# Interleaving the steps of a fixed-point feed-forward over three rows on VectorE and ScalarE

## The reference, cut to what matters

```
def float2fix(x, mantissa_bits):
    s = jnp.float32(2.0 ** mantissa_bits)
    q = jnp.round(x * s) / s
    return x + jax.lax.stop_gradient(q - x)

def pwlin_gelu_basic(x, mantissa_bits_in, mantissa_bits_out):
    xq = float2fix(x, mantissa_bits_in)
    y = jnp.interp(xq, _PWL_X, _PWL_Y)
    y = jnp.where(xq > 4.0, xq, jnp.where(xq < -4.0, jnp.float32(0.0), y))
    return float2fix(y, mantissa_bits_out)
h = jnp.einsum('bsd,df->bsf', x, w1) + b1
h = float2fix(h, 8)
h = pwlin_gelu_basic(h, 8, 8)
h = float2fix(h, 8)
out = jnp.einsum('bsf,fd->bsd', h, w2) + b2
return float2fix(out, 8)
...
x = x + _L1_ffn_ref(_layernorm(x, axis=-1), L1_ffn_w1, L1_ffn_b1, L1_ffn_w2, L1_ffn_b2)
return x
```

## Time and profile before

| | before |
|---|---|
| median of 3 runs | 2263.24 us (2263.04 to 2269.09) |
| the profiled execution | 2266.41 us |
| its span, first to last instruction | 2264.6 us |
| mean granted TensorE clock | 0.933 |
| busy share PE / DVE / ACT / POOL | 87% / 72% / 44% / 30% |
| the block that the change touches, with the store | 2126.3 to 2264.6 us of the span |

### The profile page before, as it was taken

One profiled execution on the slowest core, in us unless ns is written; L12 is line 12 of the kernel. 1 busy time (PEld: TensorE's weight loads), 2 busy tenths in 40 slices (PEclk: granted clock), 3 DMA queues, 4 the chain that ended last, 5 costly groups with the idle time before them and its releaser, 6 DMA issues. The chain is left out here.

```text
span 2264.6 us, 44140 instructions
## 1 busy us (share of the span) xinstructions
PE 1973.3 (87%) x17797; PEld 1085.4 (48%) x17800; DVE 1633.7 (72%) x2842; ACT 994.9 (44%) x1404; POOL 679.4 (30%) x704
## 2 busy tenths in 40 slices
PE   4799999999588356899999999999999999767896
PEld 1355555555445222355555555555555555434542
DVE  4399999999654794477777777777777776446676
ACT  2399998989410321233333333333333333202332
POOL 1344454444310450023332333333333332121010
PEclk8899999999699567999999999999999999988898
DMA  4133322332120401000000000000000000110400
GB/s 141 51 91 94 94 72 70 94 95 57 29 112 31 171 0 37 21 22 21 21 21 21 21 21 22 21 21 21 22 21 22 21 2 2 48 70 0 154 0 19
DMA packets 40091, 106.16 MB, mean 47 GB/s; under 512 B 19281, under 2 KB 21585, under 8 KB 33745
## 3 DMA queue, kind: packets, MB, share of 16 engines
q1 hardware_dynamic: 39888, 103.35, 14.8%
HBM read 75.42 MB, written 1.05 MB: 34 GB/s over the span
## 5 line engine op out<-in xcount | busy, mean ns | idle before, releaser
L1352 POOL TENSOR_SCALAR a1c_p_hi<-a1c_pf 128x512 f16<-128x512 f32 x272 | 201.6, 742 | 666.0 <-ACT a1c_pf L1408 623.5
L403 POOL TENSOR_SCALAR a0c_p_hi<-a0c_r 128x1024 f16<-128x1024 f32 x128 | 154.6, 1208 | 282.4 <-DVE a0c_r L492 279.5
L1377 ACT ACTIVATE a1c_k_hi<-PS 128x512 f16<-128x512 f32 x136 | 81.2, 597 | 326.8 <-PE PS L1214 326.8
L497 DVE TENSOR_TENSOR a0c_p_lo<-a0c_r,a0c_p_hi 128x1024 f16<-128x1024 f32 x128 | 202.4, 1581 | 0.9 <-POOL a0c_p_hi L403 0.9
L1557 DVE TENSOR_TENSOR a1c_p_lo<-a1c_pf,a1c_p_hi 128x512 f16<-128x512 f32 x272 | 198.2, 730 | 6.0 <-POOL a1c_p_hi L1352 6.0
L1408 ACT ACTIVATE a1c_pf<-PS,a_maskc 128x512 f32<-128x512 f32 x256 | 175.1, 686 | 48.9 <-PE PS L1719 39.0
L1384 ACT ACTIVATE a1c_v_hi<-PS 128x512 f16<-128x512 f32 x136 | 81.6, 600 | 258.8 <-PE PS L1224 206.0
L1500 DVE CUSTOM_DVE_ANT_0 a1c_junk<-PS,a1c_maskr 128x512 bf16<-128x512 f32 x256 | 175.8, 687 | 18.4
L492 DVE TENSOR_TENSOR a0c_r<-PS,a0c_r 128x1024 f32<-128x1024 f32 x128 | 155.3, 1213 | 24.9 <-ACT a0c_r L452 24.7
L1475 DVE SCALAR_TENSOR_TENSOR a1c_k_lo<-PS,a1c_k_hi 128x512 f16<-128x512 f32 x136 | 93.8, 689 | 106.3 <-ACT a1c_k_hi L1377 106.3
L1482 DVE SCALAR_TENSOR_TENSOR a1c_v_lo<-PS,a1c_v_hi 128x512 f16<-128x512 f32 x136 | 94.0, 691 | 86.7 <-ACT a1c_v_hi L1384 85.3
(11 more groups left out here) (357 smaller groups left out, 4791.7 us busy)
## 6 DMA issues: line engine op xcount, KB each, us to landing
a_cf<-in_ctxT SPq DMA_DIRECT2D x16, 1024.0 KB, 5.2
a0c_ks<-a0c_k_hi SPq DMA_DIRECT2D x128, 128.0 KB, 2.4
a1c_cf<-in_ctx SPq DMA_DIRECT2D x16, 1024.0 KB, 4.8
a0c_ks<-a0c_k_lo SPq DMA_DIRECT2D x64, 128.0 KB, 2.4
f_w<-in_w SPq DMA_DIRECT2D x4, 1024.0 KB, 8.7
f_w<-in_w SPq DMA_DIRECT2D x1, 4096.0 KB, 19.8
s1q_w<-in_L1a_wT SPq DMA_DIRECT2D x3, 1024.0 KB, 7.6
w_gate_raw<-in_w_gate SPq DMA_DIRECT2D x1, 2816.0 KB, 9.5
```

The costliest lines, as they stand in the source:

```text
L403: nc.gpsimd.tensor_scalar(p_hi[:, u % 4, :], r[:, u % 4, :], 1.0, 0.0, ALU.mult, ALU.add)\
L497: nc.vector.tensor_tensor(p_lo[:, u % 4, :], r[:, u % 4, :], p_hi[:, u % 4, :], ALU.subtract)\
L1352: nc.gpsimd.tensor_scalar(p_hi[:, v % 4, :], pf[:, v % 2, :], 1.0, 0.0, ALU.mult, ALU.add)\
```

## The change

It rewrites the feed-forward's block:

- Slots: `u` gets four, the other four tiles three. TensorE now runs `output` four rows behind `hidden` (`LAG`), and signals `outputs` after each batch of the last row.
- VectorE's list is three parts that belong to three rows. `whole(n - 2)` is the last step of row n - 2, `segment(n)` the first four of row n, `between(n - 1)` the middle three of row n - 1.
- ScalarE's list in step n: `grid(n + 1)` (scale and bias), `ends(n)` (two GELUs and, new, a Relu that makes the excess over the table), `nearest(n - 1)` (rounding).
- GpSimd's 16 steps go away: `u` is held in units of a segment (`ONE / GRID`), so that one VectorE step (`K`, L2166) both shifts and rounds, and the GELUs take off the rounding constant by their bias. VectorE's `max` goes away (now the Relu). So a row has 8 steps on VectorE instead of 9, 5 on ScalarE instead of 4, none on GpSimd.
- VectorE treats each output batch as soon as its own matmul is done, and SyncE stores each batch on its own, 256 KB each, in the same block. The block with the one store is gone; the clearing of semaphores now comes after the store.

```
-                for f in range(FT1 + 3):
+                        if f == FT1 - 1:
+                            mm.then_inc(outputs, 1)
+                for f in range(FT1 + LAG):
                     if f < FT1:
                         hidden(f)
-                    if f >= 3:
-                        output(f - 3)
+                    if f >= LAG:
+                        output(f - LAG)
...
+                def grid(f):
+                    act.wait_ge(product, f + 1)
+                    if f >= 4:
+                        act.wait_ge(y_done, f - 3)
+                    nc.scalar.activation(u[:, f % 4, :], g.PS[:, f % 4, :], ACT.Identity, bias=b1s[:, f:f + 1],
+                                         scale=ONE / GRID).then_inc(u_done, 1)
+                def ends(f):
+                    i = f % 3
+                    act.wait_ge(k_done, f + 1)
+                    if f >= 3:
+                        act.wait_ge(y_done, f - 2)
+                    nc.scalar.activation(g0[:, i, :], k[:, i, :], ACT.Gelu, scale=0.25, bias=low[:, 0:1])\
+                        .then_inc(g0_done, 1)
+                    nc.scalar.activation(g1[:, i, :], k[:, i, :], ACT.Gelu, scale=0.25, bias=high[:, 0:1])\
+                        .then_inc(g1_done, 1)
+                    nc.scalar.activation(u[:, f % 4, :], u[:, f % 4, :], ACT.Relu, scale=GRID, bias=knee[:, 0:1])\
+                        .then_inc(hm_done, 1)
+                def nearest(f):
+                    act.wait_ge(y4_done, f + 1)
+                    nc.scalar.activation(g0[:, f % 3, :], g0[:, f % 3, :], ACT.Copy, scale=ONE, bias=ROUND)\
+                        .then_inc(yr_done, 1)
+                grid(0)
+                act.wait_ge(based, 3)
+                for n in range(FT1 + 1):
+                    if n + 1 < FT1:
+                        grid(n + 1)
+                    if n < FT1:
+                        ends(n)
+                    if n >= 1:
+                        nearest(n - 1)
...
-                for f in range(FT1):
-                    i = f % R
-                    pool.wait_ge(c_done, f + 1)
-                    nc.gpsimd.tensor_scalar(k[:, i, :], c[:, i, :], 1.0 / 64, -31.5 / 64, ALU.mult, ALU.add)\
-                        .then_inc(ka_done, 1)
...
+                def segment(f):
+                    U, C, K = u[:, f % 4, :], c[:, f % 3, :], k[:, f % 3, :]
...
+                    nc.vector.tensor_scalar(K, C, -31.5 / GRID, ROUND, ALU.add, ALU.add).then_inc(k_done, 1)
...
+                for n in range(FT1 + 2):
+                    if n >= 2:
+                        whole(n - 2)
+                    if n < FT1:
+                        segment(n)
+                    if 1 <= n <= FT1:
+                        between(n - 1)
+                dve.wait_ge(biased, 2)
                 for b in range(B):
+                    dve.wait_ge(outputs, b + 1)
...
+            @block.sync
+            def _(sp):
+                for b in range(B):
+                    sp.wait_ge(x_done, b + 1)
+                    sp.dma_start(out[b], g.x[:, b, :]).then_inc(stored, 16)
+                sp.wait_ge(stored, 16 * B)
```

More of the change, by code:

```diff
@@ L2029, in _, with fixed_point_ffn_1 @@
                             normalise((n - 6) // 2)
-def fixed_point_ffn_1(nc, g, d):
+def fixed_point_ffn_1(nc, g, d, out):
+    GRID = 64.0
+    GROUND = ROUND / GRID
     ONE = 256.0
+    LAG = 4
     with ExitStack() as ctx:
@@ L2043, in fixed_point_ffn_1 @@
         w1, w2 = m.sb("w1", [P, KT, F1]), m.sb("w2", [P, FT1, D])
-        b1, b1s, b2, b2s, quarter = m.sb("b1", [P, FT1]), m.sb("b1s", [P, FT1]), m.sb("b2", [P, D]), m.sb("b2s", [P, D]), m.sb("quarter", [P, 1])
+        b1, b1s, b2, b2s = m.sb("b1", [P, FT1]), m.sb("b1s", [P, FT1]), m.sb("b2", [P, D]), m.sb("b2s", [P, D])
+        low, high, knee = m.sb("low", [P, 1]), m.sb("high", [P, 1]), m.sb("knee", [P, 1])
         w2_in, b_in = m.sem("w2_in"), m.sem("b_in")
@@ L2053, in fixed_point_ffn_1 @@
         y = m.sb("y", [P, FT1, D])
-        R = 2
-        u, c, k, g0, g1 = (m.sb(n, [P, R, D]) for n in ("u", "c", "k", "g0", "g1"))
+        u = m.sb("u", [P, 4, D])
+        c, k, g0, g1 = (m.sb(n, [P, 3, D]) for n in ("c", "k", "g0", "g1"))
         o = m.sb("o", [P, B, D])
-        based, product, u_done, h_done, c_done, ka_done, k_done, t_done = (m.sem(n) for n in (
-            "based", "product", "u_done", "h_done", "c_done", "ka_done", "k_done", "t_done"))
+        based, biased, product, u_done, h_done, c_done, k_done, t_done = (m.sem(n) for n in (
+            "based", "biased", "product", "u_done", "h_done", "c_done", "k_done", "t_done"))
         g0_done, g1_done, rise_done, td_done, y4_done, yr_done, hm_done, y_done = (m.sem(n) for n in (
             "g0_done", "g1_done", "rise_done", "td_done", "y4_done", "yr_done", "hm_done", "y_done"))
-        outputs, o_done, or_done, x_done = m.sem("outputs"), m.sem("o_done"), m.sem("or_done"), m.sem("x_done")
+        outputs, o_done, or_done, x_done, stored = (m.sem(n) for n in ("outputs", "o_done", "or_done", "x_done", "stored"))
         with nc.Block() as block:
+            @block.sync
[4 more added lines that the diff above has]
+                sp.wait_ge(stored, 16 * B)
             @block.tensor
@@ L2090, in _ @@
             @block.scalar
             def _(act):
-                act.wait_ge(based, 3)
[L2093 to L2114, removed]
-                for f in range(FT1):
-                    first(f)
-                    ends(f)
-                    last(f)
+                act.wait_ge(biased, 1)
+                def grid(f):
[4 more added lines that the diff above has]
+                                         scale=ONE / GRID).then_inc(u_done, 1)
@@ L2120, in _ @@
             @block.gpsimd
             def _(pool):
-                nc.gpsimd.memset(quarter[:], 0.25).then_inc(based, 1)
-                for f in range(FT1):
-                    i = f % R
-                    pool.wait_ge(c_done, f + 1)
-                    nc.gpsimd.tensor_scalar(k[:, i, :], c[:, i, :], 1.0 / 64, -31.5 / 64, ALU.mult, ALU.add)\
-                        .then_inc(ka_done, 1)
+                nc.gpsimd.memset(low[:], -ROUND / 4).then_inc(based, 1)
+                nc.gpsimd.memset(high[:], 0.25 - ROUND / 4).then_inc(based, 1)
@@ L2131, in _ @@
                 dve.wait_ge(b_in, 32)
[L2132 to L2136, removed]
+                nc.vector.tensor_scalar(b1s[:], b1[:], ONE / GRID, None, ALU.mult).then_inc(biased, 1)
@@ L2143, in _ @@
-                    nc.vector.tensor_scalar(C, U, 1024.0, -1024.0, ALU.min, ALU.max).then_inc(c_done, 1)
+                    if f >= 3:
+                        dve.wait_ge(td_done, f - 2)
+                    nc.vector.tensor_scalar(C, U, 1024.0 / GRID, -1024.0 / GRID, ALU.min, ALU.max)\
+                        .then_inc(c_done, 1)
                     dve.wait_ge(c_done, f + 1)
-                    nc.vector.tensor_scalar(U, U, 1024.0, None, ALU.max).then_inc(hm_done, 1)
-                    dve.wait_ge(ka_done, f + 1)
@@ L2149, in _ @@
-                    nc.vector.tensor_scalar(K, K, ROUND, ROUND, ALU.add, ALU.subtract).then_inc(k_done, 1)
+                    if f >= 3:
+                        dve.wait_ge(g1_done, f - 2)
+                    nc.vector.tensor_scalar(K, C, -31.5 / GRID, ROUND, ALU.add, ALU.add).then_inc(k_done, 1)
                     dve.wait_ge(k_done, f + 1)
-                    nc.vector.scalar_tensor_tensor(out=C, in0=K, scalar=-64.0, in1=C, op0=ALU.mult, op1=ALU.add)\
-                        .then_inc(t_done, 1)
@@ L2154, in _, with between @@
-                    dve.wait_ge(g0_done, f + 1)
+                    nc.vector.scalar_tensor_tensor(out=C, in0=K, scalar=ROUND, in1=C, op0=ALU.subtract,
+                                                   op1=ALU.subtract).then_inc(t_done, 1)
+                def between(f):
+                    C, G0, G1 = c[:, f % 3, :], g0[:, f % 3, :], g1[:, f % 3, :]
                     dve.wait_ge(g1_done, f + 1)
@@ L2224, in program @@
             clear_semaphores(nc)
[L2225 to L2233, removed]
+        self_attention_1(nc, g, d)
+        clear_semaphores(nc)
+        fixed_point_ffn_1(nc, g, d, out)
+        clear_semaphores(nc)
 def laid_out(inputs):
```

19 lines of the change are left out of this document (8 added, 11 removed).

## The result

| | before | with the change |
|---|---|---|
| median of the runs | 2263.20 us (2263.04 to 2269.09, 4 runs) | 2243.44 us (2239.24 to 2247.14, 4 runs) |
| the profiled execution | 2266.41 us | 2244.46 us |
| its span | 2264.6 us | 2242.6 us |
| mean granted clock | 0.933 | 0.935 |

The ratio is 0.9906, interval 0.9882 to 0.9930: faster by about 21 us. The forecast of 2245.7 (ratio 0.9923) lies in the interval; but 0.9906 of the time before is 2241.9, just under the lower end, 2242.5, of the range.

The account below looks back on a forecast made before the run. The prediction took the row's cross-engine chain (7.11 us) as the bound, with TensorE's 6.87 next. Its terms, -13.4 - 2.6 - 0.85 + 0.9 - 1.6 = -17.5 us, took 2263.24 to 2245.7 us, range 2242.5 to 2251.

Parts of the forecast that it names:

- What bounds the kernel: Feed-forward loop: the chain over VectorE, GpSimd and ScalarE, 7.11 us a row, bounds it; TensorE's two groups, 6.87, come next.
- The loop, -13.4: Hidden and output matmuls: TensorE runs back to back, groups 3.433 us apart, ending at 2238.35 instead of 2251.76.
- VectorE's row: VectorE's eight steps per row plus the 0.7 us wait for ScalarE's rounding, summed to 5.47 us, under TensorE's 6.87.
- The tail: Last rows: y 15 ready at 2233.8, its output group due at 2234.9, so it holds by 1.1 us.
- rival (a): Last groups: VectorE or ScalarE 10 to 20% slower, TensorE waits; 2 to 4.5 us lost, about 2249; chance 0.09.
- Closing steps by batch, -2.6: VectorE's closing steps: the first batch's matmul is done three quarters of a group before the end, saving 2.6 us.
- The store: End of the kernel: last store of 256 KB lands in 2.7 us, between bounds 2.4 (128 KB) and 4.3 (1 MB).
- -0.85 + 0.9 - 1.6: Store: engines' meeting and clearing leave the path ahead (-0.85), return behind it (+0.9), smaller last store lands sooner (-1.6).
- the 0.4 + 0.9 reckoned: Behind the store's landing: 0.4 us seen at the end before, plus 0.9 for the clearing moved there.
- The base and the range: Whole kernel: median taken 3.2 us below the profiled execution, giving 2245.7; range 2242.5 to 2251, with 2 added below.

Follow-up runs that it names:

- e1: Changed kernel, but VectorE's and ScalarE's lists hold each row whole again; GpSimd stays out, Relu stays on ScalarE: ratio to before 0.9906, loop 112.07 us.
- e4: Changed kernel with the old store, one DMA of 1 MB in a block of its own behind the clearing: ratio to before 0.9926.
- e6: Changed kernel with the output's rounding on ScalarE, VectorE left with two closing steps per batch instead of three: ratio to before 0.9913.
- e9: Changed kernel measured once more, unaltered: ratio to before 0.9906 (0.9892 to 0.9919), loop 112.11 us.
- e2: Changed kernel with the arithmetic of before, GpSimd's step and VectorE's nine steps kept, rows interleaved: ratio to before 0.9916, loop 113.85 us.
- e8: Changed kernel with three spare tensor_scalar steps, read by nothing, in each row on VectorE: ratio to before 0.9936, loop 118.34 us.
- e15: Kernel before with only the spare transposes in the norms added: ratio to before 0.9959, loop 129.02 us.
- e5: Changed kernel with 18 spare transposes on TensorE in the layer norm ahead of this stage: ratio to before 0.9911, loop 110.46 us.
- e7: Changed kernel with both e5's spare transposes and e6's shared closing steps: ratio to before 0.9894, loop 110.42 us.
- e11: e7 with the spare transposes also in the layer norms of three earlier stages and in a fourth: 2228.64 us, ratio to before 0.9851.

## Why the prediction was right, and where it fell short

**What bounds the kernel: right.** The row's chain, 7.11 us, was the bound, TensorE's two groups, 6.87, the next one. With the change TensorE sets the pace in one piece, groups 3.43 apart.

**The loop, -13.4: right, plus a chance.** In e1, e4, e6 and e9 the loop takes 112.0 to 112.1 us, against 125.2 to 125.4 in four profiles of the kernel before: 13.3. The profiled execution of the change had 1.9 more, because the clock was up at its first hidden matmul. VectorE's row (5.47 against 5.43) was summed well.

**What earns it: not weighed.** I took the interleave and the removal of GpSimd as one step. Either alone gets a row under 6.87 (6.19 in e1, 6.37 in e2), and e1 has the whole gain of the loop without the interleave. Taking GpSimd out of the interleaved kernel turns a wait of 1.5 us in the tail (e2) into 0.9 of slack. Interleaving the kernel without GpSimd brings pace that is not used, and takes slack: 2.0 us in e1, 0.9 in e9. What it buys is a VectorE that catches up after a late start.

**The tail: the slack was right, its condition was not named.** 1.1 us forecast, 0.9 measured. But the rival (a) was priced for the last rows alone, with 1 to 2 us of waiting; e8 shows that a row 1.25 us longer starves the tail by 5.7 us, because VectorE begins late and must first catch up.

**Closing steps by batch, -2.6: right** (7.28 to 4.77 is 2.5).

**The store: the term of the sum that was mis-sized.** -0.85 + 0.9 - 1.6 = -1.55 was forecast, -2.54 measured. The last store landed in 2.0 us, less than the 128 KB copies of the earlier trace rows (2.4), which I had taken as the lower bound; they go from SBUF to SBUF, and are no bound for a store. That is 2.3 off the path instead of 1.6. And the end behind the landing came to 1.0 us instead of the 0.4 + 0.9 reckoned. The Trainium skill, DMA: Bandwidth & Descriptors, anatomy of one DMA, has a fit for another issuing path that gives an estimate of 2.6 us for these 256 KB; the measured 2.0 decides. This term makes 1.0 us of the 3.8 by which the measured gain (21.3) passes the forecast one (17.5).

**The base and the range: the step that failed.** I carried over the 3.2 us between the profiled execution and the median, took the part ahead of the loop as fixed, and gave the range 2 us below the bounds of the sum for it. The result by the ratio, 2241.9, lies 0.6 below that range. Three runs within 6 us had hidden the spread: in the later comparisons the kernel before ran from 2257.16 to 2271.46 us. It lies ahead of the loop, whose first matmul starts anywhere from 2117.35 to 2129.32 us in kernels with identical code ahead of it, and it goes with the clock: over the 49 runs of the kernel before in the four comparisons, time and mean granted clock have a correlation of -0.9 (of the 17 in the first, the fastest span, 2255.9, has 0.935, the slowest, 2269.5, 0.929). The terms as the traces show them sum to 13.4 + 2.5 + 2.5 = 18.4 us, ratio 0.9919, which is within the first interval and at the very edge of the second (0.9892 to 0.9919). About 2.9 us of the measured 21.3 are thus in no term of the sum. The two profiles that were compared differ by 3.6 us more than 18.4 through the clock at the loop's start (1.9) and the unchanged part ahead (1.6); whether the rest of the ratio is that chance in all the runs, or something systematic, stays open. The thirteen profiles can't decide it. On average the loop starts at 2124.7 us in the five with the loop of before and at 2121.7 in the eight with the new one, about what is missing, and the stretch of 246 us stands in three of the five and one of the eight; but single starts are up to 12 us apart, so that can be chance. That the tail of the kernel before is mostly longer than profiled was tried and fell.

## What to carry to other kernels

When a chain over several engines is a little longer than the busiest engine's own work, any one cut that gets it under that engine earns nearly all there is (e1 all, e2 all but 1.8 us). A second cut earns at most slack, and one that makes results later, as an interleave does, can cost some. Price the slack where it is thin: at the end, where the leading engine has run out of other work, and count from when the follower can first start, not from its pace. And before taking the spread of the runs from three of them, look whether the unchanged part of the trace starts its stages at the same time twice.

## What the runs showed of the hardware

- TensorE's wait of 6.4 us ahead of the norm's transposes costs twice: the 16 transposes took 3.68 us at clock 0.50 and 2.02 at 1.00, and the next stage's first 32 records of 128x512 took 15.8 to 16.0 us or 14.0 (e15). The same happens at other stages' starts: 64 records took 29.8 or 27.7 us. Eighteen useless transposes in the wait ahead brought the clock up in time, here in e5, e7, e11 and e15; in all norms, with the shared closing steps, they made the change another 12 us faster. That fits what the Trainium skill says (TensorE: Matmul & The Clock Gate, Part 1): throttled is the default, and activity releases it.
- A store of 256 KB from SBUF landed in 2.0 us, one of 1 MB in 4.3.
- ScalarE's steps with a bias read from SBUF start 0.61 to 0.63 us after one another and take 0.71 (2134.24, 2134.87 and 2135.48 in the changed kernel); one with a constant bias takes 0.63, and the next starts 0.53 after it. I had taken 0.63 for the Relu and 0.54 for the spacing.
